# Rows of the score maxima issued by ScalarE and the sync engine, and four filler products behind the keys in place of ten

## What is computed

```
x = x + mix(layernorm(x))                       # silu(x @ Win), a decaying scan over tokens, @ Wout
x = x + cross_attention(layernorm(x), ctx, ctx) # 16 heads of width 8, 154 keys, softmax
x = x + experts(layernorm(x))                   # 8 experts, router with 3 Sinkhorn rounds, top 2
```

## Time and profile before

| | us |
|---|---|
| median of 3 runs | 431.03 |
| the 3 runs | 431.24, 424.16, 431.03 |
| the profiled execution, its own time | 426.72 |
| span of the profiled execution | 425.0 |
| PE busy | 364.5 |
| DVE busy | 241.6 |
| ACT busy | 149.2 |
| POOL busy | 56.5 |

### The profile page before, as it was taken

One profiled execution on the slowest core, in us unless ns is written; L12 is line 12 of the kernel. 1 busy time (PEld: TensorE's weight loads), 2 busy tenths in 40 slices (PEclk: granted clock), 3 DMA queues, 4 the chain that ended last, 5 costly groups with the idle time before them and its releaser, 6 DMA issues.

```text
span 425.0 us, 6290 instructions
## 1 busy us (share of the span) xinstructions
PE 364.5 (86%) x2199; PEld 250.2 (59%) x2199; DVE 241.6 (57%) x682; ACT 149.2 (35%) x300; POOL 56.5 (13%) x85
## 2 busy tenths in 40 slices
PE   1465269779997999888998999999999999999996
PEld 0353146453454634554455436888788887888875
DVE  2374538864188653873379622766567555545553
ACT  4504404713655066104632463223332222222221
POOL 7313033382012040002000200110000000000000
PEclk9996566888999999999999999999999999999999
DMA  4201176421003220061000003000000000000000
GB/s 114 61 12 35 37 163 198 106 43 52 2 0 89 65 49 1 2 151 50 0 2 2 5 2 99 2 0 2 25 2 0 2 25 2 0 2 25 0 0 25
DMA packets 17297, 15.39 MB, mean 36 GB/s; under 512 B 4469, under 2 KB 16693, under 8 KB 16981
## 3 DMA queue, kind: packets, MB, share of 16 engines
q1 hardware_dynamic: 16885, 14.84, 13.8%
q10 hardware_dynamic: 384, 0.20, 0.2%
HBM read 11.72 MB, written 3.11 MB: 35 GB/s over the span
## 4 chain that ended last, share of the span: by engine, by line
PE 69%; DVE 15%; ACT 5%; DMA 5%; issue 3%; POOL 1%; ACTq 1%; SPq 0%; DVEq 0%; POOLq 0%
PE pS L1059 14%; DVE nmax_mask L911 5%; PE pS L1217 4%; PE pC L1232 4%; PE pS L253 4%; PE pS L255 4%; PE pS L254 4%; PE pC L1229 3%; PE pS L1214 3%; PE pA L253 3%; PE pA L255 3%; PE pA L254 3%; PE pB L253 3%; PE pB L254 3%; PE pB L255 3%
## 5 line engine op out<-in xcount | busy, mean ns | idle before, releaser
L1059 PEld LDWEIGHTS pS<-prob,sig 128*128 128x128 f32 x512 | 64.7, 191 | 13.9 <-DVE res L723 6.3
L712 DVE TENSOR_TENSOR sig<-xi_f,pS 128x512 f32<-128x512 f32 x64 | 43.9, 687 | 49.9 <-PE pS L255 44.9
L1059 PE MATMUL pS<-prob,sig 128*128 128x128 f32 x512 | 69.1, 279 | 1.2 <-DVE sig L712 1.0
L911 DVE TENSOR_REDUCE nmax_mask<-pS 128x3 f32<-128x462 f32 (+1 forms) x96 | 52.3, 575 | 12.4 <-PE pS L1184 12.3
L639 ACT ACTIVATE prob<-pS 128x512 f32<-128x512 f32 x80 | 42.1, 600 | 27.6 <-PE pS L1217 27.6
L723 DVE SCALAR_TENSOR_TENSOR res<-pS,w_gate,res 128x128 f32<-128x128 f32 (+1 forms) x128 | 36.0, 344 | 13.9 <-PE pS L1059 12.5
L556 ACT ACTIVATE xi_f<-pA 128x512 f32<-128x512 f32 x32 | 19.1, 597 | 61.0 <-PE pA L255 60.9
L1181 PE MATMUL pS<-k_stack,q_stack 72*128 72x154 bf16 x256 | 35.7, 245 | 2.0 <-DMA q_stack<-q_scr 1.9
L556 ACT ACTIVATE xi_f<-pB 128x512 f32<-128x512 f32 x32 | 19.1, 597 | 51.3 <-PE pB L255 51.2
L1184 PE MATMUL pS<-mbias,ident_bf 128*128 128x462 bf16 (+1 forms) x96 | 35.2, 367 | 0.0
L1181 PEld LDWEIGHTS pS<-k_stack,q_stack 72*128 72x128 bf16 x256 | 21.5, 105 | 10.1 <-DVE nmax_mask L911 4.1
(11 more groups left out here) (279 smaller groups left out, 670.0 us busy)
## 6 DMA issues: line engine op xcount, KB each, us to landing
q_stack<-q_scr SPq DMA_DIRECT2D x12, 384.0 KB
q_scr<-q_parts SPq DMA_DIRECT2D x12, 128.0 KB, 2.4
k_stack<-k_scr SPq DMA_DIRECT2D x36, 40.0 KB
res<-in_x_dram SPq DMA_DIRECT2D x4, 256.0 KB, 6.4
prob<-in_L_ffn_wg_dram SPq DMA_DIRECT2D x1, 1024.0 KB, 6.0
prob<-in_L_ffn_wp_dram SPq DMA_DIRECT2D x1, 1024.0 KB, 10.1
out_dram<-res SPq DMA_DIRECT2D x4, 256.0 KB, 2.2
prob<-in_L_ffn_wo_dram SPq DMA_DIRECT2D x1, 768.0 KB, 4.8
```

The lines of the kernel that those rows point to most:

```text
L712: dve.tensor_tensor(hid[:, i % 2, :], relu[:, i % 2, :], pUp[i % 2][:, :], ALU.mult).then_inc(s_hid, 1)
L911: dve.tensor_reduce(nmax[:, qt, hs[0]:hs[-1] + 1], score_bank(b, n)[:, 0:len(hs) * KEYS].rearrange("p (h k) -> p h k", k=KEYS), AX.X, ALU. ...
L1059: last = pe.matmul(pO[:, toks], hid[:, i % 2, toks], wo_sb[:, e, hf, :], start=(hf == 0 and t == 0), stop=(hf == HF - 1), skip_group_check ...
```

## The change

`max_rows` becomes a step of SP as well: it waits for ACT's copy and issues the second and the third row, while ACT issues the first only. The three DMAs still add 48 to `s_mrow`. The filler products at the end of slot 26 become four in place of ten, in each of the four images.

```diff
             for g in range(G - 1):
                 place([("weigh", b, g), ("copy_group", b, g), ("by_token", b, g), ("attn_norm", b, g)],
                       [B0 + 5 * g + n for n in GROUP_AT])
-            slots[B0 - 1] += [("keep_busy", b, 10)]
+            slots[B0 - 1] += [("keep_busy", b, 4)]
             STEPS += [step for slot in slots for step in slot]
...
                             sp.dma_start(k_stack[b % 2][r0:r0 + DK, :, :], k_scr[b][a]).then_inc(s_kst, 16)
+                elif step == "max_rows":
+
+                    sp.wait_ge(s_mTc, b + 1)
+                    for p_ in range(1, PARTS):
+                        sp.dma_start(q_stack[b % 2][MROW + p_:MROW + p_ + 1, :, :],
+                                     mT[p_ * H:(p_ + 1) * H, :]).then_inc(s_mrow, 16)
...
                     act.copy(mT[:, :], pT_bf[0:PARTS * H, 0:S]).then_inc(s_mTc, 1)
                     act.wait_ge(s_mTc, b + 1)
-                    for p_ in range(PARTS):
-                        act.dma_start(q_stack[b % 2][MROW + p_:MROW + p_ + 1, :, :],
-                                      mT[p_ * H:(p_ + 1) * H, :]).then_inc(s_mrow, 16)
+                    act.dma_start(q_stack[b % 2][MROW:MROW + 1, :, :], mT[0:H, :]).then_inc(s_mrow, 16)
```

## The result

The changed kernel takes 430.01 us (median of 20 runs, 428.3 to 433.54) against 429.49 us of the kernel before (20 runs, 424.16 to 434.18). The ratio of the two is 1.007, 95% interval 1.0045 to 1.0095, when only executions within 1.5% of each kernel's quickest are compared, which cuts off the upper part of the wide spread of before, so I give the medians of all runs beside it. By both the change is no gain, and by the ratio it is 0.7% slower: the 3 us that I forecast are not there.

What follows compares the result with a forecast made beforehand. PE carries 69% of the chain; before the scores, fillers or row landings end last. Gains of 1.3 + 0 + 1.15 + 0.65 = 3.1 us, with 3 taken off 428.9, gave 426.0 us, range 420 to 432.

Steps and rivals of the forecast that it cites:

- the 3 us that I forecast: Whole kernel: the gains of the four images sum to 3.1 us, 0.7% of the time, giving 426.0 us.
- Image 0, 1.3 us from the fillers: Before image 0's scores: fillers end last, so six fewer save six products at full clock, 1.3 us.
- The prediction set this fall beside a wait for a DMA: Window of 136 to 137 us: clock fall cited as agreeing with throttling after a DMA wait between short compute.
- Image 1, nothing: Image 1: scores begin sooner, but PE then waits for DVE's norm at 153.30; gain 0, bounds 0 and 1.4 us.
- Image 2, 1.15 us from the split: Before image 2's scores: rows end last; SP's second row lands at 192.65, gain 1.15 us, bounds 0 to 1.7.
- The prediction's limit of 0.6 us for one issue saved: Row issue: splitting saves only issuing time, at most 0.6 us an image, 2.4 us in all, where rows end last.
- Image 3, 0.65 us from the split: Before image 3's scores: last row lands at 238.3 against 239.0, gain 0.65 us, bounds 0 and 1.2.
- I take nothing: ACT and SP issuing together in images 2 and 3: price assumed zero, open up to 0.6 us in each.
- the rival to which I gave one chance in five: Fewer fillers let PE idle and its clock fall; one fall in images 1 to 3 each: 430.3 us; chance 0.20.
- the idle stretches are short and stand between dense ones: PE's idle in images 1 to 3, 1.2 to 1.7 us: argument against the clock falling there.

Runs made afterwards that it cites:

- e11: The full change again, unedited, with four fillers in every image: 430.54 us (12 runs), ratio 0.9992 to the kernel before.
- e12: The full change with 14 fillers in image 2 alone (4, 4, 14, 4 in images 0 to 3): 427.95 us, ratio 0.993 to the kernel before.
- e2: The kernel before, all rows issued by ACT, with four fillers instead of ten in every image: 430.49 us, ratio 1.0076 to the kernel before.
- e8: The kernel before with one ACT DMA for all three rows and 4, 10, 14, 8 fillers: 428.51 us, ratio 0.9929 to the kernel before.
- e16: The kernel before, unchanged, one more profiled execution: 432.07 us.
- e1: The full change with ten fillers kept in every image, so only the issue is split: 428.66 us, ratio 0.9992 to the kernel before.
- e9: The kernel before, unchanged, one more profiled execution: 427.01 us.
- e10: The kernel before, unchanged, one more profiled execution: 428.68 us.
- e4: The full change with ten fillers in images 0 and 1, four in images 2 and 3: 431.4 us (6 runs), ratio 1.0106 to the kernel before.
- e6: The full change with 4, 4, 14, 12 fillers in images 0 to 3: 425.08 us (6 runs), ratio 0.9882 to the kernel before.
- e15: The full change with 4, 4, 14, 12 fillers in images 0 to 3, same kernel as e6: 426.21 us (12 runs), ratio 0.9927 to the kernel before.
- e7: The full change with 10, 10, 14, 12 fillers in images 0 to 3: 427.18 us, ratio 0.9898 to the kernel before.
- e3: The full change with 4, 10, 14, 12 fillers in images 0 to 3: 426.72 us, ratio 0.9988 to the kernel before.
- e13: The full change with 12 fillers in image 3 alone (4, 4, 4, 12 in images 0 to 3): 427.4 us, ratio 1.0023 to the kernel before.
- e14: The kernel before, all rows issued by ACT, with 4, 4, 16, 12 fillers in images 0 to 3: 429.01 us, ratio 0.9975 to the kernel before.
- e5: The kernel before, all rows issued by ACT, with 4, 10, 16, 12 fillers: 426.91 us (6 runs), ratio 0.989 to the kernel before.

## Why the prediction was wrong

I went by these steps; the measured values are from the first profile after, unless another is named.

- **Image 0, 1.3 us from the fillers: right.** The scores start 4.22 us after the copy in place of 5.77, 1.55 us sooner. (Four fillers at the full clock take 1.04 us and not 4 x 0.217 = 0.87, because the last one takes 0.38: the prediction forgot that in images 1, 2 and 3, by 0.2 us.) The stretch to image 1 got shorter by 2.64. The other 1.1 us I put down to a fall that before had from about 136.7 to 140.1 and this execution of the change did not; e11 and e12, with the same four fillers, had one there (of 7 us) and took 49.3 us for the stretch. The fillers may still have a hand in it: all seven profiles with ten fillers in image 0 have a fall in that place, of the eleven with four only five. The prediction set this fall beside a wait for a DMA; the 1.08 us for which PE stood in front of it were ended by POOL (line 529).
- **Image 1, nothing: right.** 43.24 against 43.23 us. The scores start 3.95 us after the copy in place of 5.00; the last row sets that and not the fillers, because SP's second issue begins only 1.58 us after the start of the copy (1.19 in images 2 and 3). And the idle time in front of the transpose stands in the timeline, 1.20 us where I had 1.4.
- **Image 2, 1.15 us from the split: half of it.** 5.40 against 6.05, so 0.65. Over all profiles the start lies at 5.30 to 5.83 with the split and at 5.48 to 6.74 with ACT alone. So the split is worth something in this image, where ACT's second and third issues take 1.05 to 2.55 us each, but 0.65 is one pair of executions: against e2, at 5.48, it is 0.08. The prediction's limit of 0.6 us for one issue saved does not hold for this image by its own rows, in which the second issue took 1.31 us.
- **Image 3, 0.65 us from the split: 0.10.** Here my choice "I take nothing" for two engines issuing at the same moment failed. The lines of the two issues and their landings in image 3 after, of line 634 (ACT) and then line 450 (SP):

```profile
L634 ACTq DMA_DIRECT2D q_stack<-mT x1: 512/512/512, 234.8 to 234.8; - x1
DMA to landing us min/median/max: 2.7/2.7/2.7
...
L450 SPq DMA_DIRECT2D q_stack<-mT x2: 546/696/847, 234.8 to 235.4; - x2
DMA to landing us min/median/max: 2.1/2.4/2.7
```

ACT's row and SP's second land after 2.7 us, not 2.2, and SP's second issue lasts 0.85 us, not 0.6. One issue of 0.6 us is saved and 0.5 us of landing is added. ACT's row takes 2.7 to 2.8 in images 0, 1 and 3 of every profile with the split, and ACT's three rows take 2.1 to 2.3 each in every one without, e8 aside. The Trainium skill (DMA: Bandwidth & Descriptors, "Issuing engines are not separate DMA queues") names the issuing time as all that can be saved; the trace agrees, and in image 3 even that was nearly all given back.

- **The step that decided: the clock.** The direct terms add up to 1.55 + 0 + 0.65 + 0.10 = 2.3 us for 3.1 predicted. That they do not show in the time is the rival to which I gave one chance in five. I had its places, images 2 and 3, and its price. What I had wrong is the sentence "the idle stretches are short and stand between dense ones". Of the 18 profiles five have four fillers in image 2 and five in image 3; the clock fell within 2 us of the scores' start in four of the five each time. Of the 13 others each time, it fell there in none in image 3, and in image 2 only in e16, where PE stood equally long (2.1 us). The longest idle without a fall is 1.65 us in image 3 (e12) and 1.97 in image 2 (e11); idles of 1.06 to 1.76 us in image 2 (before, e1, e9, e10) and of 1.08 in image 3 (e8) had none either. What changed is the idle in front: from 0.4 to 1.6 us in image 3, from 1.4 to 2.1 in image 2. The two falls behind the scores' start cost about 3.0 us by the price below, more than the 2.3 gained.

**The price of a fall**, from the stretches. From the copy of image 3 to the end it takes 189.8 to 190.2 us in the nine profiles with no fall between the start of the scores and the last few microseconds, 191.5 with one of 3.5 us, and 192.9 to 193.1 with two such, or with one of 7 us as in e2, e4 and e11. So 3.5 us of half clock cost 1.5 us. From the copy of image 2 to that of image 3, with the split: 46.64 with no fall (e6), 47.57 to 48.53 with one (e15, e11, e7, e3), 49.05 to 49.79 with two (e12, e1, e4, change, e13): 0.9 to 1.9 each. My 1.4 to 1.65 lies inside that. In the change's profile the two stretches lose 2.50 + 2.94 us by four falls, less the 0.75 us gained; two of the four are those behind the scores' start. The other two begin at 200.8 and, among the experts, near 282.8, each right behind the 24 small products of a router (see the last section). Executions of other kernels have such falls too, e9, e10 and e16 of before among them, and no run ties them to the change.

**What stays open.** The runs of before move over 10 us, and the profiles tie the differences to falls in images 0 and 2 and among the experts, but I have only four of its executions in profile, none of those at 424. Every timed execution has its mean granted clock on record, and it goes with the time: in the 29 runs of before beside e1 the two quickest, 424.32 and 424.8 us, have 0.946 and 0.942, and the five with 0.911 or 0.912 all take 433.15 us or more (correlation of time and clock -0.64 there, -0.77 to -0.80 in the other groups). Whether the split with cover is really quicker than ACT alone with cover (2.8 us by the medians of e15 and e14), when the start of the scores explains 0.4 us in image 2 and 0.25 in image 3, isn't settled: e5, also ACT alone, was as quick as e3, and the profile of e14 has falls of 7 and 3.4 us between the copies of images 2 and 3 and two of 3.4 us behind them, that of e15 one of 3.4 us in each stretch, none of them at the start of the scores. What makes one execution fall at a place and the next not (e11 in image 2, e12 in image 3) wasn't tried.

## What to carry to other kernels

Filler work in front of a wait can be there to hold TensorE's clock, and then it is to be sized until the wait really ends and not until it is no longer on the chain: here six products less freed nothing in images 2 and 3 and were followed by one to two more falls of about 1.5 us each. Where a saving shortens the cover by more than it shortens the wait, add up both before taking the saving. And a second issuing engine is worth its issue time only if the transfers then land as fast as one at a time; measure the landing, not the issue.

## What the runs showed of the hardware that I had not expected

- Two engines issuing small DMAs at the same moment: in images 0, 1 and 3 ACT's row lands 0.6 to 0.7 us later than its first row of before (2.7 to 2.8 in place of 2.1 to 2.2), though ACT's DMAs go on q10 and SP's on q1 and, in image 3, no other transfer is issued.
- While 1.15 MB moves on SP's queue, or just behind that, ACT's second and third issue of 16 KB take 1.05 to 2.55 us each in place of 0.6 (the 1.31 of the earlier trace rows and the 2.55 of e16 among them); its first stays at 0.53. SP's own issues in the same place stay at 0.55 to 0.68 us.
- One DMA of 48 KB into three partitions takes 3.6 us (e8, image 3), three of 16 KB into one each 3.3 together.
- The clock can fall right behind work that reads as dense. In the change's profile it fell behind 24 products of only 8 columns each, back to back. The first and the last of them in the timeline, and two windows of the clock:

```profile
197.61 0.36 PE L253 MATMUL pB<-rwT_hi,x_hi 128*128 128x8 f32 x1
...
200.28 0.25 PE L255 MATMUL pB<-rwT_hi,x_lo 128*128 128x8 f32 x1
```

```profile
199.00:200.00 1.00, 1.00 (x11) 1.00 (x10) 0.00 (x0) 0.00 (x0) 0.00 (x0) 1.00 0.00 0
201.00:202.00 1.00, 1.00 (x5) 0.55 (x3) 0.53 (x3) 0.67 (x2) 0.00 (x0) 0.50 0.00 0
```

PE is shown as busy all the time, and from 200.8 on the clock is at half. A fall at this place is frequent: it began within 1.5 us of the end of these 24 products in 14 of the 18 profiles in image 2, and in 6 of the 18 behind the same 24 of image 3. The four without it in image 2 are before, e10, e6 and e15. No run changed these products, so that they are the cause is likely and not shown.
